# A fused cross-attention and soft-MoE kernel: loads of the first batch reordered, the rest of the layernorm moved, and the last token group's combine rewritten

## The reference

```python
# attention
xn = layernorm(x)
q, k, v = xn @ Wq, ctx @ Wk, ctx @ Wv          # 16 heads of 64
attn = softmax(q k^T / 8)                      # over the 1500 context rows
x = x + (attn v) @ Wo
# soft MoE
x2n = layernorm(x)
logits = x2n @ phi_w^T + phi_b                 # tokens x (64 experts x 32 slots)
D = softmax(logits, over the 32 slots of an expert)
C = softmax(logits, over the 64 experts)       # for each slot number
X = clip(sum_tokens D * x2n);  X = tanh(layernorm(X))
Y = X @ expert_w + expert_b
x = x + sum_slots C * Y
```

## Time and profile before

| | |
|---|---|
| median of 3 executions | 431.97 us (431.68 to 433.04) |
| the profiled execution | 429.94 us, of which the span of the instructions is 428.2 us |
| busy | PE 98%, DVE 78%, ACT 57%, POOL 40% of the span |
| granted TensorE clock | 1.00 of full speed |
| chain that ended last | PE 73%, DVE 17%, ACT 7% of the span |

### The profile page before, as it was taken

One profiled execution on the slowest core, in us unless ns is written; L12 is line 12 of the kernel. 1 busy time (PEld: TensorE's weight loads), 2 busy tenths in 40 slices (PEclk: granted clock), 3 DMA queues, 4 the chain that ended last, 5 costly groups with the idle time before them and its releaser, 6 DMA issues.

```text
span 428.2 us, 7420 instructions
## 1 busy us (share of the span) xinstructions
PE 417.8 (98%) x2973; PEld 383.4 (90%) x2973; DVE 335.8 (78%) x615; ACT 245.0 (57%) x412; POOL 170.1 (40%) x99
## 2 busy tenths in 40 slices
PE   7999999999999999999999999999999999999897
PEld 5888999999999999889999998899999888999787
DVE  4788756776886778767898689978988899669981
ACT  3577547664664546654673766466655564645541
POOL 5419701424450405032608053617146543456710
PEclk9999999999999999999999999999999999999999
DMA  7410110213020011110020001001000000396000
GB/s 197 144 27 10 41 51 14 63 43 96 14 48 38 20 14 18 69 18 14 14 73 20 12 14 72 21 12 15 0 20 12 2 12 20 54 259 181 2 2 23
DMA packets 15418, 19.05 MB, mean 44 GB/s; under 512 B 4032, under 2 KB 10960, under 8 KB 15384
## 3 DMA queue, kind: packets, MB, share of 16 engines
q1 hardware_dynamic: 15384, 18.57, 17.0%
HBM read 18.31 MB, written 0.26 MB: 43 GB/s over the span
## 4 chain that ended last, share of the span: by engine, by line
PE 73%; DVE 17%; ACT 7%; DMA 1%; issue 1%; SPq 0%; ACTq 0%
PE turned L735 14%; PE acc L755 8%; PE acc L757 7%; PE acc L756 7%; PE scores L719 7%; PE scores L725 7%; PE scores L722 7%; DVE small L1411 5%; DVE pT_l L1421 4%; ACT prob L1167 4%; PE misc L772 3%; PE misc L641 2%; PE scores L1097 2%; ACT pT_h L1160 1%; PE misc L800 1%; ACT logit L1218 1%
## 5 line engine op out<-in xcount | busy, mean ns | idle before, releaser
L1160 ACT CAST pT_h<-turned 125x512 fp32r<-125x512 f32 x168 | 95.2, 590 | 123.6 <-PE turned L735 122.9
L1421 DVE TENSOR_TENSOR pT_l<-turned,pT_h 125x512 fp32r<-125x512 f32 x168 | 112.4, 686 | 56.7 <-ACT pT_h L1160 55.9
L1411 DVE TENSOR_REDUCE small<-scores 128x1 f32<-128x500 f32 x168 | 107.9, 673 | 3.7 <-PE scores L725 3.3
L735 PE MATMUL turned<-ident,prob 128*125 128x128 f32 x672 | 94.4, 276 | 2.0 <-DVE pT_l L1421 1.7
L735 PEld LDWEIGHTS turned<-ident,prob 128*125 128x125 f32 x672 | 87.5, 187 | 9.7 <-DVE pT_l L1421 3.9
L755 PE MATMUL acc<-pT_h,ctx_nh 125*128 125x256 f32 (+1 forms) x288 | 95.0, 330 | 0.0
L1167 ACT ACTIVATE prob<-scores,small 128x1500 f32<-128x1500 f32 x56 | 84.9, 1517 | 10.9 <-DVE small L1414 10.7
L757 PE MATMUL acc<-pT_h,ctx_nl 125*128 125x256 f32 (+1 forms) x288 | 86.5, 300 | 0.0
L756 PE MATMUL acc<-pT_l,ctx_nh 125*128 125x256 f32 (+1 forms) x288 | 86.4, 300 | 0.0
L719 PE MATMUL scores<-ctx_th,qk_h 128*128 128x500 f32 x168 | 70.3, 419 | 0.4 <-ACT prob L1167 0.4
L725 PE MATMUL scores<-ctx_th,qk_l 128*128 128x500 f32 x168 | 65.3, 389 | 0.0
(11 more groups left out here) (212 smaller groups left out, 552.5 us busy)
## 6 DMA issues: line engine op xcount, KB each, us to landing
ctx_raw<-in_ctx_dram SPq DMA_DIRECT2D x7, 750.0 KB
rbc<-rden_row SPq DMA_DIRECT2D x15, 128.0 KB, 3.5
rbc<-rden_row SPq DMA_DIRECT2D x8, 192.0 KB, 3.0
eb<-in_L_ffn_expert_b_dram SPq DMA_DIRECT2D x4, 256.0 KB, 6.0
ctx_raw<-in_ctx_dram SPq DMA_DIRECT2D x3, 224.0 KB, 5.3
wq_sb<-in_L_xattn_Wq_dram SPq DMA_DIRECT2D x2, 256.0 KB, 4.6
wk_sb<-in_L_xattn_Wk_dram SPq DMA_DIRECT2D x2, 256.0 KB, 5.3
wv_sb<-in_L_xattn_Wv_dram SPq DMA_DIRECT2D x1, 512.0 KB, 3.6
```

Source lines behind the costliest of these rows:

```text
L735: last = tr(turned[0:CK, m, 128 * c:128 * c + 128], prob[u][:, CK * j:CK * j + CK], ident[:, :])
L1160: nc.scalar.copy(pT_h[0:CK, PLACES[g // NT % 2][t], CPB * k:CPB * k + CPB, :], turned[0:CK, (KB * u + k) % 2, :].rearrange("p (c r) -> p c ...
L1411: m = v.tensor_reduce(bankmax[:, u, k:k + 1], scores[:, k, 0:KW], AX.X, ALU.max)
L1421: v.tensor_tensor(pT_l[0:CK, place, dst, :], turned[0:CK, (KB * u + k) % 2, :].rearrange("p (c r) -> p c r", c=CPB), pT_h[0:CK, place, dst ...
```

## The change

It has six parts.

1. SP loads only token group 0 of x first, then the halves of Wk and Wq (Wk ahead of Wq), then the whole first context in two DMAs (112 rows, 13 rows) where it had four, then the second weight halves, the rest of x, Wv and Wo without a wait between.
2. PE does the head products of the first half ahead of the first two context turns; `keep_busy` is six narrower matmuls and one more behind `turn_xn`. ACT and DVE follow that order (`lo_qk` stands ahead of the second `lo_ctx` on DVE).
3. The statistics of token groups 1 to 3 of x move on DVE to t = 3 of batch 0, and on POOL their root and the normalised x move behind `split_weights`.
4. The last group's logits are stored slot by slot (experts innermost) by `copy_logits`, so that the maximum and the sum over experts read adjacent words in one instruction each; the scale reads them back with a stride and writes expert by expert into the tile `disp_104`.
5. In the tail ACT does `tanh_slots(2)` ahead of `combine_exp(LAST)`, and DVE does its half of the shift behind `add_expert_bias(0)`.
6. `combine` for groups 0 to 2 is turned round: the expert outputs are the weights and 336 token columns stream. The result is token-last, so it is copied by ACT (`y2T`) and turned back by three transposes (`turn_y2`), between the rounds of `combine_last`.

```diff
-            sp.dma_start(x_sb[:, :, :], x_v).then_inc(x_in, 16)
+            sp.dma_start(x_sb[:, 0:1, :], x_v[:, 0:1, :]).then_inc(x_in, 16)
+            sp.dma_start(wk_sb[:, 0:HW], Wk[:, 0:HW]).then_inc(wk_in[0], 16)
             sp.dma_start(wq_sb[:, 0:HW], Wq[:, 0:HW]).then_inc(wq_in[0], 16)
-            sp.dma_start(wk_sb[:, 0:HW], Wk[:, 0:HW]).then_inc(wk_in[0], 16)
-            sp.dma_start(ctx_raw[ROWS0:CK, :, :], ctx_v[0][ROWS0:CK, :, :]).then_inc(ctx0_rest_in, 16)
-            for k in range(KB):
-                chunks = slice(CPB * k, CPB * k + CPB)
-                sp.dma_start(ctx_raw[0:ROWS0, chunks, :], ctx_v[0][0:ROWS0, chunks, :]).then_inc(ctx0_in[k], 16)
+            for n, (p0, p1) in enumerate(ROW_PARTS):
+                sp.dma_start(ctx_raw[p0:p1, :, :], ctx_v[0][p0:p1, :, :]).then_inc(ctx0_in[n], 16)
             sp.dma_start(wq_sb[:, HW:INNER], Wq[:, HW:INNER]).then_inc(wq_in[1], 16)
             sp.dma_start(wk_sb[:, HW:INNER], Wk[:, HW:INNER]).then_inc(wk_in[1], 16)
-            sp.wait_ge(ctx0_in[KB - 1], 16)
+            sp.dma_start(x_sb[:, 1:NQ, :], x_v[:, 1:NQ, :]).then_inc(x_rest_in, 16)
             sp.dma_start(wv_sb[:, :], Wv).then_inc(wvo_in, 16)
...
             root(0, 0, 1)
+            split_ctx(0, 0, first=True)
+            split_qk(1)
+            split_weights()
             root(1, 1, NQ)
             pool.wait_ge(ln_rs, 2)
             for q in range(1, NQ):
                 last = gp.tensor_scalar(xn[:, q, :], x_sb[:, q, :], lnmv[:, q, 0:1], lnrs[:, q:q + 1],
                                         ALU.subtract, ALU.mult)
             last.then_inc(xn_rest, 1)
-            split_ctx(0, 0, first=True)
-            split_qk(1)
-            split_weights()
             split_ctx(1, 1)
             split_xa()
...
-            turn_xn(0, 1, ACC)
-            turn_ctx(0, 0, 1, first=True)
+            turn_xn(0, 1, M0)
+            keep_busy(1)
             pe.wait_ge(setup_act, 1)
             pe.wait_ge(setup_dve, 1)
             head_pairs(wqT, wkT, 0, T1, S1)
+            turn_ctx(0, 0, 1, first=True)
+            pe.wait_ge(xnT_dve, 1)
             turn_ctx(0, 1, 0, first=True)
...
+            def combine(r):
+                pe.wait_ge(yt_dve, r + 1)
                 for k in range(4 * r, 4 * r + 4):
-                    for q in range(q0, q1):
-                        last = mm(bank(SLOT_BANKS[part])[0:PT, H * (q - q0):H * (q - q0) + H],
-                                  combT[:, k, PT * q:PT * q + PT], yt[:, k, :],
-                                  start=(k == 0 and q == q0), stop=(k == NS - 1), skip_group_check=True)
+                    last = mm(bank(S0)[:, 0:LAST * PT], yt[:, k, :], combT[:, k, 0:LAST * PT],
+                              start=(k == 0), stop=(k == NS - 1))
...
+            combine_last(0)
+            combine_last(1)
+            turn_y2()
+            combine_last(2)
+            combine_last(3)
...
             dve.wait_ge(x_in, 16)
             layernorm(0, x_sb, 0, 1)
-            layernorm(1, x_sb, 1, NQ)
             layernorm_apply(0, x_sb, xn, 0, 1, xn_ready)
...
                     if first and t == 3:
                         copy_out(14, wvo[:, 9:16:2, :], M1)
+                        dve.wait_ge(x_rest_in, 16)
+                        layernorm(1, x_sb, 1, NQ)
...
+            def last_combine_scale(r):
+                dve.wait_ge(crec_dve, LAST + 1)
+                src = comb[LAST][:, :].rearrange("p (s n) -> p n s", n=N_EXP)[:, EPB * r:EPB * r + EPB, :]
+                v.tensor_tensor(by_expert(comb_by_expert[LAST][:, QUARTER * r:QUARTER * r + QUARTER]), src,
+                                csum[LAST][:, :].unsqueeze(1).broadcast_to([PT, EPB, P_SLOT]),
                                 ALU.mult).then_inc(comb_dve, 1)
```

More of the change, by code:

```diff
@@ L231, in xattn_softmoe_kernel @@
         setup_dve = sem("setup_dve")
-        ctx0_in = [sem(f"ctx0_in{k}") for k in range(KB)]
-        ctx0_rest_in = sem("ctx0_rest_in")
+        ctx0_in = [sem(f"ctx0_in{n}") for n in range(2)]
         ctx_in = sem("ctx_in")
@@ L437, in split_ctx @@
                 if first:
-                    pool.wait_ge(ctx0_rest_in, 16)
-                    for k in range(KB):
-                        pool.wait_ge(ctx0_in[k], 16)
+                    for part_in in ctx0_in:
+                        pool.wait_ge(part_in, 16)
                 else:
@@ L1107, in _ @@
             experts(1)
-            combine(0, 0)
+            combine(0)
             turn_xt(2)
-            combine(0, 1)
+            combine(1)
             experts(2)
             turn_xt(3)
-            combine(0, 2)
+            combine(2)
             experts(3)
             turn_comb(LAST)
-            combine(0, 3)
-            for r in range(4):
-                pe.wait_ge(combT_act, 12 + r + 1)
-                combine(1, r)
+            combine(3)
+            combine_last(0)
[3 more added lines that the diff above has]
+            combine_last(3)
         @block.scalar
@@ L1355, in _ @@
             copy_combT(LAST)
+            act.wait_ge(y2_pe, 1)
+            nc.scalar.copy(y2T[:, :], bank(S0)[:, 0:LAST * PT]).then_inc(y2T_act, 1)
         @block.vector
```

115 lines of the change are left out of this document (69 added, 46 removed).

## The result

The changed kernel takes 433.8 us (median of 15 runs, 431.83 to 435.72) against 431.23 us (15 runs of the kernel before on the same chip): a ratio of 1.0066, 95% interval 1.0050 to 1.0082. It is slower, by 2.6 us. The profiled execution took 433.8 us, with a span of 432.0 us and a mean granted TensorE clock of 0.996.

The account below looks back on a forecast made before the run. PE, 98% busy, was taken to bound the attention, and chains through DVE, ACT, POOL and DMA the head and tail. Span 428.2 - 0.4 + 3.1 - 1.6 = 429.3, 1.1 more; on 431.97 about 433.0 us, range 430.7 to 434.6.

Parts of the forecast that it names:

- my own case: Whole kernel: the forecast itself, 432.2 to 433.5 us, nearly all within 0.3% of before; chance 0.38.
- The head: Program start: products earlier, context landing at 8.6, first reduction at about 12.6 against 12.98; 0.4 us gained.
- (a): First batch, t = 3: seven statistics instructions on DVE, about 1.1 us, cost PE 0 to 0.5 us, taken as 0.
- (b) to (d): First batch: POOL's 3.37 us shift delays `load_ctx(2)` and the denominators' DMA behind it; PE loses 3.1 us (2.2 to 3.4).
- the other two places: PE, batch 1: `turn_probs` needing `pT_l`, 2.9 us lost, and `ahead_head` needing its copied bank, 3.1 us lost.
- The clock: PE's new stall of about 2 us: rival that the slow rate returns, 2 us more, 435; chance 0.04.
- The tail: After the last logits: shorter reductions, earlier round 3 turn and wide combines, less three transposes; 1.6 us gained (0.8 to 2.5).
- the context lands late: Head, `turn_ctx(0, 0)`: rival that the first context lands after 8.6; at 9.4 it costs 0.8 us, 433.9; chance 0.30.
- the shift doesn't reach DVE: First batch: rival that SP's DMAs land independently, so DVE's wait doesn't grow; 430.0 us, faster; chance 0.14.
- the ends gain more: Head and tail: rival that these gain more or the denominators' wait is smaller; 430.9 us at its bounds; chance 0.14.

Follow-up runs that it names:

- e11: Kernel before with the changed loads and order of the head, statistics of pairs 1 to 3 at step 0, tail of before: 431.84 us, ratio 1.0005.
- e1: Kernel before with only POOL's root and three normalisations moved behind `split_weights`: 434.79 us, ratio 1.0078.
- e4: Kernel before with the tail's parts of the change alone (logits layout, tanh and shift order, wide combine): 429.35 us, ratio 0.9958.
- e6: Kernel before with POOL's root and normalisations behind `split_weights`, and SP's third context load behind the denominators' DMAs: 431.22 us, ratio 1.0002.
- e7: Kernel before with one more DVE instruction, `lnvar` computed again while POOL is inside `wqk_h`: 433.43 us, ratio 1.0063.
- e8: Kernel before with the tail's parts of the change and SP's third context load behind the denominators' DMAs: 429.19 us, ratio 0.9933.
- e2: Changed kernel with the addition of epsilon for token groups 1 to 3 done on POOL instead of DVE: 433.91 us, ratio 1.0060.
- e12: Changed kernel with that addition of epsilon on POOL and SP's third context load behind the denominators' DMAs: 429.14 us, ratio 0.9928.
- e3: Changed kernel with SP waiting for the first context before it issues the rest of x, Wv and Wo: 433.25 us, ratio 1.0038.

## Why the prediction came out as it did

The time of 433.8 us lies in the range, 0.8 above the 433.0 forecast, but that is luck in two ways. The forecast was 1.1 us on top of 431.97, the median of 3 executions; the median of 15 is 431.23. So the difference was forecast at 1.1 us and measured at 2.57, and a base 0.74 too high brought the sum closer. And the mechanism that cost the time is not the one forecast: `oT` has no idle time for `rbc` in front of it, where 4.8 us were forecast. The direction was given less than it deserved: I held a difference within 0.3% for the likeliest, and it is 0.66%, outside the 432.2 to 433.5 of my own case.

**The head, -0.4 us: about 0.** The step of this term that failed is the landing of the context: 8.6 assumed, 10.49 in the profile, 9.18 to 10.51 over seven profiles of the new load. But the price of the late landing isn't read from one profile of each. Over six profiles with the code of the old head the first reduction starts at 12.98 to 15.17 (mean 14.07), over seven with the new head at 13.12 to 15.06 (mean 14.12), and e11 agrees, within its interval, that they are worth the same. The 12.98 of the earlier trace rows was a lucky execution: the head products took 0.27 us each in it and in e1, 0.42 in the other four (e4, e6, e7, e8), and of the old heads only those four start their reductions after 14. The products are 1.56 times as long, though the window rows give a granted clock of 1.00 in both; what sets their rate isn't shown. The new head pays with a later landing, and gets back products that were fast in six of seven. Where the landing is late it can cost a fall of the clock besides (e2).

**(a) The statistics at t = 3, 0 taken with 0 to 0.5 as bounds: 4.4 us.** This is the step that failed: 2.67 us of stall and 1.71 by the clock, for a term put at nothing. I priced the seven instructions by their own durations and asked only whether DVE had room. I didn't ask what POOL was doing at that time. `lnvar` takes 0.15 to 0.17 us wherever POOL is idle, and lasts to the end of POOL's instruction where it starts inside a long one (3.57 in the changed kernel, 2.71 in e7). The Trainium skill (SBUF — State Buffer, section "Who interferes with whom") states this as an exclusive lock: DVE's two-port modes, which a `tensor_scalar` with its operands in SBUF can enter, and GpSimd's instructions share a pair of ports, and the second to issue waits for the whole of the first. The trace agrees in the times: in both kernels the instruction ends within 0.03 us of POOL's, and e7 shows it alone. That it is the ports that are locked no run here can show. By this page the price could have been put at up to 3.6 us, an estimate: the length of `wqk_h`.

**(b) to (d) The denominators, 3.1 us with 2.2 to 3.4 as bounds: right as a mechanism, but not what the changed kernel pays.** e1 shows each link: the load at 52.37, `rbc` at 61.75, DVE waiting 4.93 us, PE stopped. The term was mis-sized: 2.27 us of stall, which is the lower bound where only the first wait counts, and 1.71 by the clock, 4.02 together. PE stood once, at `context_product`, and not again at the other two places. e6 shows by its reverse that the queue is the cause. In the changed kernel (a) makes DVE and PE so late that the wait is hidden. The two don't add: the denominators alone cost 4.0 us (e1), and the changed kernel with both 4.5, of which (a) accounts for 4.38. A kernel with (a) alone wasn't run. That is why e2, which removed only the first, gained nothing, and e12, which removed both, 4.8 us.

**The clock, a rival at 0.04: it happened, though at another place.** In the first two batches stalls of 2.27 (e1), 2.66 (e3), 2.67 (changed) and 2.99 us (e2) were followed by a granted clock of 0.50 and a loss of 1.71 us each time, near the 2 us that this rival gave. In the head 2.47 us (e2) were followed by a fall that cost 1.70, and 2.25 us (e3) and 1.89 us (changed) by none; in e7 1.52 us were followed by none. That 2.25 and 2.27 us end differently, and that two of the 15 executions of the changed kernel keep a clock of 1.000, suggests that the length of the stall isn't all of it; what else decides stays open. I gave it so little because no such stall was in the trace, though the forecast itself put one there. The Trainium skill (TensorE: Matmul & The Clock Gate, Part 1) says that an idle PE loses its full clock, and in the changed kernel, e1, e2 and e3 it did.

**The tail, -1.6 us: -2.0.** Every term was there. Round 3's turn is 1.14 us earlier (1.0 forecast). The next combine starts 0.46 us behind it instead of 0.88, so 0.42 (0.2). Two wide combines gain 0.44 and 0.36 (0.35 each). From there to the last `out_sb` it is 0.34 longer (0.35). Sum 2.02. The strided scale takes 3.92 us, the upper end of my 2.5 to 3.9, and is hidden: PE turns `comb` without a wait. (The extra that the forecast drew from the stride, 1.3 us, is 1.39 by its own figures; measured are 3.92 - 2.49 = 1.43.) ACT's strided copies of the logits take 1.03 to 1.06 us and delay nothing.

**The sum.** 0 + 4.5 - 2.0 = 2.5 us, against 2.57 between the medians. The 4.5 is of an execution with one fall of the clock, the commonest kind of the 15.

**The rivals.** That the context lands late was true, and didn't decide: its price of 0.1 us for each 0.1 us held in the profile (the landing 1.89 us later than forecast, the first reduction 1.78), but the old head starts as late on average. That the shift doesn't reach DVE is refuted by e1. In the changed kernel it doesn't stop DVE, because (a) has made DVE later still. That the ends gain more is true of the tail, by 0.4 us; the head gave that much less.

## What to carry to other kernels

A cheap instruction has no price of its own: before it is moved, look at what the other engine that shares its ports runs at that time, and at what is queued behind it. Where two delays fall on one chain, removing the first may only uncover the second; test them apart and together. And read a stage that varies from execution to execution from several profiles: marks that are in every kernel (here the first reduction, the last `x2l` and the end) showed where the time went (371.27 to 371.38 us of attention in eight kernels without a loss, 371.66 in the ninth, e11), while the head alone varied by 2 us. See also how far the profiled execution is from the median.

## What the hardware showed that I had not expected

- A DVE `tensor_scalar` on 112 x 3 elements took 3.57 us next to a POOL instruction of 3.60 us, and 0.17 without. The two `bn` instructions ahead of it and DVE's reductions out of PSUM ran beside POOL at their usual times (1.83 and 1.84 us for three), and so did its copy of 128 x 512 out of PSUM (0.69 us).
- PE stalls of 2.27 to 2.99 us, at a PE otherwise busy, were followed by a granted clock of 0.50 that cost 1.71 us in each of four kernels; one of 1.52 us by none. In the head one of 2.47 us was followed by such a fall, one of 2.25 us not.
- In the head, the same products took 0.27 or 0.42 us each by execution, with a granted clock that reads 1.00 in both.
- ACT's copy of 112 x 512 took 1.03 to 1.06 us with a strided destination, 0.57 with adjacent words.
